# GpSimd's indirect transfers group by group, and the weights loaded beside the constants, in a four-layer graph network

## The reference, cut to what matters

```python
agg = segment_sum(h[src], dst); h = relu(agg @ W.T + b)                      # layer 0
ef = concat([x[row], x[col], edge_attr_2]); h = relu(batch_norm(ef @ W1 + b1))
out = segment_sum(h @ W2 + b2, row) / (counts + 1) + x                       # layer 1
logits = sum(q[dst] * (k[src] + e)) / 4; alpha = segment_softmax(logits, dst)
agg = segment_sum(alpha * (v[src] + e), dst)                                 # layer 2, then an FFN
score = exp(leaky_relu(src_score[src] + tgt_score[dst]) - max); ...          # layer 3, weighted sum by dst
```

## Time and profile before

| | us |
|---|---|
| median of 3 runs | 6624.19 (6605.84 to 6630.1) |
| the profiled execution | 6624.27 |
| its span in the trace | 6622.5 |
| PE busy | 5189.9 (78%) |
| DVE busy | 4327.9 (65%) |
| ACT busy | 2747.1 (41%) |
| POOL busy | 4019.6 (61%) |
| mean granted TensorE clock | 0.907 |

### The profile page before, as it was taken

How to read it: one execution, slowest core, us unless ns; L and a number is a source line. 1 busy time by engine, 2 the same in 40 slices (tenths; PEclk the granted TensorE clock), 3 DMA queues, 4 the chain that set the end, 5 groups by cost and what they waited for, 6 DMA issues and landing times. The chain is left out here.

```text
span 6622.5 us, 108943 instructions
## 1 busy us (share of the span) xinstructions
PE 5189.9 (78%) x29030; PEld 3716.2 (56%) x29030; DVE 4327.9 (65%) x15755; ACT 2747.1 (41%) x6645; POOL 4019.6 (61%) x3613
## 2 busy tenths in 40 slices
PE   4777799868886666487868999969898967776798
PEld 3655577744555555433337888735555535555576
DVE  4554677733335555477757888869999955555698
ACT  0000355521111111266643555557777742222355
POOL 4666366666666888677765545315555555544699
PEclk9899899978888788799988999989999978888999
DMA  4555566634445666699974555434444423333476
GB/s 129 169 176 168 155 184 178 172 108 133 131 130 109 106 106 106 117 310 312 302 226 132 149 148 149 116 98 128 131 127 132 127 73 72 74 72 71 127 199 185
DMA packets 1159174, 966.37 MB, mean 146 GB/s; under 512 B 156342, under 2 KB 970882, under 8 KB 1158564
## 3 DMA queue, kind: packets, MB, share of 16 engines
q1 hardware_dynamic: 977956, 684.36, 34.4%
q0 software_dynamic: 158368, 210.14, 15.7%
q10 hardware_dynamic: 22240, 64.90, 2.6%
HBM read 485.30 MB, written 496.79 MB: 148 GB/s over the span
## 5 line engine op out<-in xcount | busy, mean ns | idle before, releaser
L526 POOL DMA_INDIRECT tgt_tab<-l_nodes_ext,rank_at x392 | 452.8, 1155 | 411.4 <-ACT l_nodes_ext L2328 308.6
L1563 POOL DMA_INDIRECT agg<-l_edges_b_rows,l_edges_b_at x392 | 608.6, 1552 | 135.5 <-issue 76.8
L1851 POOL DMA_INDIRECT l_edges_kv<-kv_tab,src_i x392 | 399.6, 1019 | 401.7 <-DVE l_edges_v_e L1872 292.9
L2526 POOL DMA_INDIRECT l_edges_proj<-proj_tab,src_i x392 | 381.8, 974 | 384.0 <-DVE l_edges_msg L2499 254.2
L526 POOL DMA_INDIRECT to_col<-l_nodes_col_s,rank_row x392 | 415.0, 1059 | 323.5 <-ACT l_nodes_col_s L1257 213.8
L968 POOL DMA_INDIRECT l_edges_fetched<-in_x,src_i x392 | 382.6, 976 | 218.9 <-DMA dst_i<-in_dst 111.6
L898 ACT COPY l_edges_rows<-l_edges_sums 128x264 f32<-128x264 f32 (+1 forms) x294 | 122.1, 450 | 944.6 <-DMA dst_i<-in_dst 462.3
L1321 POOL DMA_INDIRECT l_edges_a_at_row<-to_row,src_i x392 | 378.9, 967 | 218.3 <-issue 111.4
L526 POOL DMA_INDIRECT q_tab<-l_nodes_qkvs,rank_at x392 | 401.7, 1025 | 147.4 <-issue 110.7
L851 DVE TENSOR_SCALAR l_edges_hot<-columns,local_edge 128x128 f32<-128x128 f32 (+3 forms) x784 | 257.6, 380 | 295.3 <-DMA dst_i<-in_dst 285.5
L1733 PE MATMUL l_nodes_y<-w_qkvs,l_nodes_x_t 128*128 128x512 f32 x784 | 419.5, 617 | 0.0
(11 more groups left out here) (364 smaller groups left out, 14451.4 us busy)
## 6 DMA issues: line engine op xcount, KB each, us to landing
agg<-zeros ACTq DMA_DIRECT2D x98, 516.0 KB
l_nodes_xg<-x SPq DMA_DIRECT2D x196, 256.0 KB
kv_tab<-l_nodes_qkvs SPq DMA_DIRECT2D x98, 512.0 KB
agg<-l_edges_rows SPq DMA_DIRECT2D x98, 266.0 KB
l_nodes_ag<-agg SPq DMA_DIRECT2D x98, 266.0 KB
proj_tab<-l_nodes_ext SPq DMA_DIRECT2D x98, 264.0 KB
l_nodes_ag<-agg SPq DMA_DIRECT2D x98, 258.0 KB
l_nodes_ag_odd<-agg SPq DMA_DIRECT2D x98, 258.0 KB
```

What stands on the lines that cost most here:

```text
L526: pool.indirect_dma_start(table, bass.IndirectOffsetOnAxis(ranks[:, n * G + j:n * G + j + 1].bitcast(U32), 0), rows[:, j, :], None, bounds ...
L1563: pool.indirect_dma_start(agg1[j // 2], bass.IndirectOffsetOnAxis(at[k][:, j:j + 1].bitcast(U32), 0), rows[k][:, j, :], None, compute_op=A ...
L1851: pool.indirect_dma_start(kv[k][:, j, :], None, kv_tab, bass.IndirectOffsetOnAxis(src_i[:, n * G + j:n * G + j + 1].bitcast(U32), 0),).the ...
L2526: pool.indirect_dma_start(proj[k][:, j, :], None, proj_tab, bass.IndirectOffsetOnAxis(src_i[:, n * G + j:n * G + j + 1].bitcast(U32), 0),) ...
```

## The change

Ahead of the four transfers of group n, POOL waits until the transfer of the last tile (j = 3) of group n - 1 has landed: in `gather_sum_edges`, `edges_1a` and `edges_3`, and in the helper `scatter`, which `nodes_0`, `nodes_1` and `nodes_2` call. `edges_1b` and `edges_2` keep what they have. The older waits stay, ahead of the new one. The 37 weight transfers are issued in `load_consts`, behind `dst` and `src`, and `load_weights` waits for nothing but their arrival. The 16 mask transfers leave SP and `rank_rows`; ACT issues them at the start of `gather_sum_edges`, where they are waited for at the end. The tiles `reset_s`, `open_s`, `w0` and `attend` live through the whole program.

```diff
@@@ scatter_steps, one of four like it (the others wait on gathered, row_in and proj_in)
                 n = place(i, k)
                 pool.wait_ge(ready, count)
                 pool.sem_inc(turn, 1)
+                if n:
+                    pool.wait_ge(out[(n - 1) % RING][G - 1], (n - 1) // RING * 16 + 16)
                 for j in range(G):
                     pool.indirect_dma_start(
@@@ load_consts
                     def _(dve):
+                        dve.memset(attend[:], 0.0).then_inc(zero_made, 1)
                         dve.memset(zeros[:], 0.0).then_inc(zero_made, 1)
-                        dve.wait_ge(zero_made, 1)
+                        dve.wait_ge(zero_made, 2)
...
                         sp.dma_start(dst_i[:], dst).then_inc(loaded[0], 16)
                         sp.dma_start(src_i[:], src).then_inc(loaded[1], 16)
+                        begin_weights(sp, zero_made)
                         for s in loaded:
                             sp.wait_ge(s, 16)
@@@ rank_rows
-                            dve.tensor_scalar(open_s[:], open_s[:], 0.0, NEVER, ALU.is_gt, ALU.mult).then_inc(masked, 1)
+                            chain(dve.tensor_scalar(open_s[:], open_s[:], 0.0, NEVER, ALU.is_gt, ALU.mult))
...
-                        if last_of is not None:
-                            sp.wait_ge(masked, 1)
-                            for table, mask in ((reset_tab, reset_s), (open_tab, open_s)):
-                                for h in range(H2):
-                                    sp.dma_start(table[:, h, :], mask[:]).then_inc(mask_out, 16)
-                            sp.wait_ge(mask_out, 2 * H2 * 16)
@@@ gather_sum_edges, fetch
+                            if n:
+                                pool.wait_ge(gathered[(n - 1) % RING][G - 1], (n - 1) // RING * 16 + 16)
@@@ gather_sum_edges, ACT
+                        for table, mask in ((reset_tab, reset_s), (open_tab, open_s)):
+                            for h in range(H2):
+                                act.dma_start(table[:, h, :], mask[:]).then_inc(cleared, 16)
                         rotation(act, groups, (0, lambda i, k: empty(act, i, k)), (0, clear), loop=False)
-                        act.wait_ge(cleared, 16 * (2 * pairs + 2))
+                        act.wait_ge(cleared, 16 * (2 * pairs + 2 + 2 * H2))
@@@ new, called in load_consts
+        def begin_weights(sp, cleared):
+            for to, frm in plain:
+                sp.dma_start(to, frm).then_inc(weights_in, 16)
+            with nc.allow_non_contiguous_dma(reason="short columns, once"):
+                for to, name in short:
+                    sp.dma_start(to[:], column(name)).then_inc(weights_in, 16)
+                sp.wait_ge(cleared, 2)
+                for m, name in enumerate(("L3_gnn_a_src", "L3_gnn_a_tgt")):
+                    for h in range(H3):
+                        sp.dma_start(attend[h * C3:(h + 1) * C3, m * H3 + h:m * H3 + h + 1],
+                                     w[name][0, h, :].rearrange("(c a) -> c a", a=1)).then_inc(attend_in, 16)
@@@ load_weights
                     def _(dve):
-                        dve.memset(attend[:], 0.0).then_inc(cleared, 1)
-                        dve.wait_ge(loaded, total)
+                        dve.wait_ge(weights_in, total)
```

More of the change, by code:

```diff
@@ L410, in gnn @@
         comes_in, goes_on = sb0("comes_in", [1, groups]), sb0("goes_on", [1, groups])
+        reset_s, open_s = sb0("reset_s", [groups, GE]), sb0("open_s", [groups, GE])
+        weights_in, attend_in = nc.alloc_semaphore(name="weights_in"), nc.alloc_semaphore(name="attend_in")
         closing = sb0("closing", [P, groups])
@@ L650, in rank_rows @@
                 line_s = sb("line_s", [groups, 2, GE], BF16)
-                reset_s, open_s = sb("reset_s", [groups, GE]), sb("open_s", [groups, GE])
                 own_p, whole_p = ps("own_p", [P, 512]), ps("whole_p", [P, 512])
@@ L654, in rank_rows @@
                 line_p = ps("line_p", [P, 512])
-                step, summed, ranked, placed, lined, copied, line_out, masked, mask_out = (
-                    sem(n) for n in ("step", "summed", "ranked", "placed", "lined", "copied", "line_out", "masked", "mask_out"))
+                step, summed, ranked, placed, lined, copied, line_out = (
+                    sem(n) for n in ("step", "summed", "ranked", "placed", "lined", "copied", "line_out"))
                 numbered, in_lines, turned = sem("numbered"), sem("in_lines"), sem("turned")
@@ L1020, in gnn, with row, column @@
         bn_scale, bn_shift = sb0("bn_scale", [P, 1]), sb0("bn_shift", [P, 1])
+        w0, attend = sb0("w0", [P, D]), sb0("attend", [P, 2 * H3])
+        def row(name):
+            return w[name].rearrange("(a n) -> a n", a=1).to_broadcast([P, D])
+        def column(name, m=1):
+            return w[name].rearrange("(m p) -> p m", p=P)
+        plain = [(w0[:], w["L0_gnn_W"]), (w1_ab[:, 0:D], w["L1_gnn_W1"][0:D, :]),
+                 (w1_ab[:, D:2 * D], w["L1_gnn_W1"][D:2 * D, :]), (w1_c[:], w["L1_gnn_W1"][2 * D:2 * D + 2, :]),
+                 (w1_2[:], w["L1_gnn_W2"]), (w_e[:], w["L2_gnn_We"]), (w_f1[:], w["L2_gnn_Wf1"]),
+                 (w_f2[:], w["L2_gnn_Wf2"].rearrange("(c p) n -> p c n", p=P)),
+                 (w_proj[:, 0:D], w["L3_gnn_W_proj"]),
+                 (b_0[:], row("L0_gnn_b")), (b_11[:], row("L1_gnn_b1")), (b_12[:], row("L1_gnn_b2")),
+                 (g_2[:], row("L2_gnn_g2")), (b_2[:], row("L2_gnn_b2")),
+                 (b_3[:], row("L3_gnn_bias"))]
+        for m, n in enumerate(("q", "k", "v", "skip")):
+            plain.append((w_qkvs[:, m * D:(m + 1) * D], w[f"L2_gnn_W{n}"]))
+            plain.append((b_qkvs[:, m * D:(m + 1) * D], row(f"L2_gnn_b{n}")))
+        short = [(gamma, "L1_gnn_gamma"), (beta, "L1_gnn_beta"), (g_1, "L2_gnn_g1"), (b_1, "L2_gnn_b1"),
+                   (b_f1, "L2_gnn_bf1"), (b_f2, "L2_gnn_bf2")]
+        total = 16 * (len(plain) + len(short))
+        def begin_weights(sp, cleared):
[9 more added lines that the diff above has]
+                                     w[name][0, h, :].rearrange("(c a) -> c a", a=1)).then_inc(attend_in, 16)
         def split_row(dve, space, row, parts, ready, count, name):
@@ L1046, in load_weights @@
                 sb, ps, sem, free = space
-                w0, proj_t, attend = sb("w0", [P, D]), sb("proj_t", [P, D]), sb("attend", [P, 2 * H3])
+                proj_t = sb("proj_t", [P, D])
                 turned, mixed = ps("turned", [P, 2, P]), ps("mixed", [P, 2 * H3])
-                loaded, cleared, attend_loaded = sem("loaded"), sem("cleared"), sem("attend_loaded")
                 s_turned, s_copied, s_mixed, s_done = sem("s_turned"), sem("s_copied"), sem("s_mixed"), sem("s_done")
-                def row(name):
-                    return w[name].rearrange("(a n) -> a n", a=1).to_broadcast([P, D])
@@ L1065, in load_weights @@
-                for m, n in enumerate(("q", "k", "v", "skip")):
-                    plain.append((w_qkvs[:, m * D:(m + 1) * D], w[f"L2_gnn_W{n}"]))
-                    plain.append((b_qkvs[:, m * D:(m + 1) * D], row(f"L2_gnn_b{n}")))
-                columns = [(gamma, "L1_gnn_gamma"), (beta, "L1_gnn_beta"), (g_1, "L2_gnn_g1"), (b_1, "L2_gnn_b1"),
-                           (b_f1, "L2_gnn_bf1"), (b_f2, "L2_gnn_bf2")]
-                total = 16 * (len(plain) + len(columns))
-                with nc.Block() as block:
-                    @block.sync
-                    def _(sp):
-                        for to, frm in plain:
-                            sp.dma_start(to, frm).then_inc(loaded, 16)
-                        with nc.allow_non_contiguous_dma(reason="short columns, once"):
-                            for to, name in columns:
-                                sp.dma_start(to[:], column(name)).then_inc(loaded, 16)
-                            sp.wait_ge(cleared, 1)
-                            for m, name in enumerate(("L3_gnn_a_src", "L3_gnn_a_tgt")):
-                                for h in range(H3):
-                                    sp.dma_start(attend[h * C3:(h + 1) * C3, m * H3 + h:m * H3 + h + 1],
-                                                 w[name][0, h, :].rearrange("(c a) -> c a", a=1)).then_inc(attend_loaded, 16)
-                        sp.wait_ge(loaded, total)
-                        sp.wait_ge(attend_loaded, 16 * 2 * H3)
```

22 lines of the change are left out of this document (8 added, 14 removed).

## The result

Beside each other on one chip the kernel before took 6620.05 us (median of 4 runs, 6605.84 to 6630.1) and the kernel after 7057.94 (4 runs, 7046.36 to 7064.75): a ratio of 1.066, 95% interval 1.065 to 1.068, so slower, as forecast, but by 438 us where the forecast's sum had 211. The time lies just above the range.

The account below looks back on a forecast made before the run. POOL's transfer issues, plus other engines' messages held back by back-to-back issuing, were taken to set the pace. Five stages' terms summed to 2.28 us a group, times 98 = +223; less 12 at the start, 6835, say 6840 us; range 6590 to 7040.

Parts of the forecast that it names:

- the mechanism that the forecast gave for it: Five stages: each group's first transfer waits for the previous group's fourth landing, idle 2.0 to 2.7 us that nothing hides.
- The start: Start-up: weight issues moved behind src and masks moved to ACT save 14.3 us, less 2 for mask traffic: -12.
- Layer 1's edges: Layer 1 edge stage: less traffic, so quiet idle time of 2.02 us; 6.71 against 5.98 us a group, +0.73.
- Layer 3's edges: Layer 3 edge stage: wait releases held-back messages, POOL's own 6.98 us becomes the pace, -0.74 a group.
- the term of layer 1's nodes: Layer 1 node stage: slow landing under DMA share 0.90, idle time 2.7 us; 7.49 against 6.45, +1.04 a group.
- Four transfers d us long: Five stages: a group's four transfers, d each, hold POOL for 4d + 0.90, 4.69 to 4.84 us.
- x: Five stages: POOL's idle time between groups beyond 4d + 0.90; after the change bounded by 1.55 and 2.60 us.
- x = 2.28 in both layer 0 stages: Layer 0 edges and nodes: idle time equals the mean of 49 earlier waits; +0.83 and +0.42 a group.
- The start-up after a real wait: POOL, from landing to next transfer's start: between 0.30 and 0.77 us, taken as 0.77.
- the first rival: The wait is cheap: POOL starts 0.30 us after the landing, 184 us less in four stages, 6650; chance 0.20.
- The 1.83 us of the reader: Layer 3's edges: end of the fourth issue to DVE's reader starting, taken as the landing in x's upper bound.
- The slow one: Slow landings: x = 2.60, 4.0 in layer 1's nodes, layer 3's edges gain nothing; 7155 us, chance 0.12.

Follow-up runs that it names:

- start_only: Kernel after with all four new waits taken out, leaving the moved weight and mask transfers: 6030.68 us beside 6042.86 for the kernel before, 0.998.
- pause_b: Kernel after without new waits; POOL runs one iota ahead of each group's transfers in layer 0's and layer 3's edges: 6566.62 us beside 6580.36 (kernel before).
- start_l3_b: Kernel after keeping only layer 3's edge wait and the moved weights and masks: 6519.13 us beside 6580.36 (kernel before); first run, start_l3, 6209.16 beside 6038.15.
- traffic2: Kernel after, SP's loads and stores to kv_tab and skip_tab in layer 1's nodes cut to a quarter of the rows: 7135.47 us, some 190 for filling tables.
- traffic: Kernel after, zeroing moved from layer 0's to layer 1's edges, kv_tab store in layer 1's nodes cut to a quarter: 7163.04 us, some 120 for filling.
- turn: Kernel after with POOL's sem_inc moved behind the new wait, so no transfer stands directly behind it: 7228.16 us.

## Why the prediction was right and wrong

**Right.** The direction, and the mechanism that the forecast gave for it: fours, each followed by idle time that a landing ends, in all five stages. The start: -12 forecast, -13.4 in the trace, -12 in start_only; the weights' issues end at 19.4 (19.3 forecast), and the masks on ACT cost nothing that is seen. Layer 1's edges (+61 for +72), where the idle time of 1.85 for 2.02 us and the transfers of 0.964 for 0.947 us err in opposite ways. Layer 3's edges (-64 for -73), and that this gain came from a release: pause_b and start_l3_b show it.

**Wrong: the term of layer 1's nodes**, "between 2.02 and 5.0 I take 2.7, a quarter of the way", +1.04 a group. It is 8.94 - 4 x 1.067 - 0.90 = 3.77 us idle and +2.49 a group. "With the queue empty ahead of each group it should be much less" was the faulty step: POOL's queue is empty then, SP's is not. A landing shares the engines with the loads and stores of all queues, and traffic2 took back 1.05 us by cutting SP's. This is (3.77 - 2.7) x 98 = 105 us of the excess. The 5.0 us of the earlier trace rows were no good bound: they come from a trace with the holding in it, and are near the longest that the kernel after shows from issue end to landing (5.28 us, mean 2.97). Half way between the bounds would have been 3.5.

**Wrong: d was a median.** "Four transfers d us long" took 0.947, 0.985, 0.972, 0.947 and 0.95; the means after are 0.969, 1.032, 1.067, 0.964 and 1.017. Four times the differences, over 98 groups, make 9 + 18 + 37 + 7 + 26 = 97 us. Most of it could be had from rows 1, where 414.98 us over 392 transfers is 1.059: with the means before (0.976, 1.059, 1.025, 0.967, 0.974) the same sum is 78. The rest is a rise in layer 1's nodes and layer 3's edges, against slightly shorter transfers elsewhere, that nothing ahead of the run showed. In the split of the kernel before that did not show, since x was the remainder; in the sum of a new period it does.

**Wrong, with little net:** x = 2.28 in both layer 0 stages, which came to 2.56 and 2.61. The zeroing in every second group (traffic) makes it in the edges, in the nodes a landing of 1.81 us with the writes' start-up of 0.78. Against that, layer 1's and layer 3's edges have 0.17 us less than their 2.02 and 2.28. The start-up after a real wait, taken as 0.77, is 0.26 us where the read itself bears the wait, and 0.76 with an increment between (turn). There the first rival, with 0.30, was right; for the writes, with 0.78, the forecast's 0.77 was. The 1.83 us of the reader in rows 5 is no bare landing either: the quiet landing takes 1.59, and the rest would be the reader's own start. The Trainium skill, page "Perfetto Trace Analysis", section "DMA Instruction — SWDGE (GPSIMD)", says that the decoded instruction sits in a wait queue until its semaphores are satisfied; this trace agrees for the reads (0.26 us against 0.76 with an increment between).

**The rivals.** The slow one, at 7155, came nearer than the forecast: its 2.60 in the layer 0 stages and its 4.0 in layer 1's nodes stand beside 2.56, 2.61 and 3.77. It was wrong in layer 1's edges (1.85) and in giving layer 3's edges no gain. The forecast's remark that "a third to a quarter of the stage seems free" is off for layer 3's edges, where the earlier trace rows has POOL busy for 382 of 757 us; no term rests on it.

**Not foreseen.** That the kernel before has two times. On an occasion without the holding the change costs 1017 us: the five stages then lose 30 to 49% each, layer 3's edges among them (701 us for 526). In the three edge stages POOL's issues set the pace there, 0.30 us apart from first to last, and every wait is added to it. The forecast argued from a trace with the holding in it and treated that as the kernel's own pace.

**What stays open:** what decides whether a run has the holding. The same chip had it in one comparison and not in another, and within a comparison all runs agreed (17 runs of 6027 to 6053, 13 of 6612 to 6642). The halved number of recorded semaphore updates names a rival that nothing here tests: that taking the trace plays a part in the holding. Every time on record comes with the span of a trace, so no run shows what the two kernels take without one. Why the windows of other stages give 15 us back is not settled either; `edges_1b`'s transfers take 731 us in both.

## What to carry to other kernels

A wait for one's own landing, ahead of every batch, adds the whole of it to the period of an engine that has nothing else to do: cost it as mean issue time plus the landing under the stage's real traffic, all queues counted, plus the start-up behind it (0.26 or 0.78 us here), and take means, not medians, for the terms of a sum. A wait for a transfer two places back mostly hides where traffic is light, and a read that itself bears the wait, with nothing between, starts soonest. Where engines hear of each other late while GpSimd issues in long runs, a wait or a short pause in the one stage that suffers can pay (some 50 us here), but run the kernel before on several occasions first: the same kernel (start_l3) was 171 us slower when there was nothing to release.

## What the runs showed of the hardware

- While GpSimd issues indirect transfers back to back, other engines' semaphore messages can come late (4.4 us in rows 4; more than 2 us in 49 of 97 groups), and a pause of 2.0 us in each group ends it (pause_b). This is there on some occasions and absent on others, for one program and even one chip: 6580 and 6043 us. The traces with it hold about half as many recorded semaphore updates (62,303 and 124,624), and whether recording has a part in it is open.
- In layer 3's edges, 757 us with the holding, a wait for half of the transfers under way releases next to nothing (742), a wait for all of them in every second group part of it (722), in every group more (701), and a pause of 2.0 us as much or more (689).
- From the end of the last issue to the next start, a 64 KB (128 rows of 512 bytes) indirect read awaited by the next transfer took 1.84 us in a quiet stage, of which 1.58 are the landing, and 4.0 beside 1 MB of zeroing; a write took 2.6 to 3.8. The Trainium skill, page "DMA: Bandwidth & Descriptors", section "Anatomy of one DMA — SWDGE (gpsimd) path", fits 2.0 us plus 436 bytes a nanosecond, which makes an estimate of 2.15 us for 64 KB. From issue start to landing it was 0.94 + 1.58 = 2.52 here when quiet, so 0.4 more than that, and the zeroing added 2.1.
- After the last update of a landing an indirect read that waits for it starts in 0.26 us, with an increment between in 0.76, and a bounds-checked write, whose register move bears the wait, in 0.78.
